# Chunk 0 prepared ahead of the last one-hot groups, and sorted rows turned by products with the identity

## What is computed

```python
xn = layernorm(x)
# branch 1: tokens sorted by nearest of 8 means, then a selective scan over the sorted order
buckets = argmax(l2norm(xn) @ l2norm(means).T);  sort_idx = argsort(buckets, stable=True)
u = xn[sort_idx].T
x_dbl = x_proj_weight @ u                       # 32 rows dts, 16 rows B, 16 rows C
C = x_dbl[48:] + (means @ prompt_weight.T)[sorted bucket].T
delta = softplus(dt_projs_weight @ dts + dt_projs_bias)
h = exp(delta * A) * h + (delta * u) * B;  y = sum_n(h * C) + D * u     # 16 states a channel
# branch 2: top-2 of 8 experts, each silu(xn @ w1) * (xn @ w3) @ w2
out = x + unsort(y) + experts(xn)
```

## Time and profile before

| | before |
|---|---|
| three runs, median (lowest to highest) | 813.2 us (810.62 to 814.56) |
| the profiled execution | 809.9 us, span 808.1 us |
| VectorE busy | 681.9 us, 84% of the span |
| TensorE busy | 656.6 us, 81% |
| GpSimd busy | 595.9 us, 74% |
| ScalarE busy | 420.7 us, 52% |
| granted TensorE clock, mean of the span | 0.914 of full speed |
| moved by DMA | 116.97 MB, mean 145 GB/s |

### The profile page before, as it was taken

The page is one execution under the profiler, slowest core; times in us unless marked ns, Lnnn a source line. Parts: engine busy times, 40 slices in busy tenths (PEclk is TensorE's granted clock), DMA queues, the critical chain, the costliest instruction groups (busy, mean ns, idle before and its releaser), DMA issues.

```text
span 808.1 us, 13714 instructions
## 1 busy us (share of the span) xinstructions
PE 656.6 (81%) x4538; PEld 422.3 (52%) x4538; DVE 681.9 (84%) x883; ACT 420.7 (52%) x910; POOL 595.9 (74%) x371
## 2 busy tenths in 40 slices
PE   2733879558988799987989898899879888989991
PEld 1423734225655465555656555565546555655661
DVE  5868767679999999999999999999989999997120
ACT  1323666546655565565555665566546555652320
POOL 3727810055698899898989998898989899898442
PEclk9955965588999999999999999999999999999996
DMA  7982568999835744674475456556536754433231
GB/s 205 370 285 91 167 215 276 294 304 258 187 87 114 172 108 92 145 167 92 107 155 118 107 131 144 118 118 144 128 78 147 158 106 100 89 61 45 47 40 20
DMA packets 66275, 116.97 MB, mean 145 GB/s; under 512 B 12104, under 2 KB 46496, under 8 KB 64160
## 3 DMA queue, kind: packets, MB, share of 16 engines
q1 hardware_dynamic: 44048, 88.78, 39.0%
q0 software_dynamic: 19824, 27.16, 19.6%
q10 hardware_dynamic: 2336, 0.15, 0.2%
HBM read 80.78 MB, written 35.27 MB: 144 GB/s over the span
## 4 chain that ended last, share of the span: by engine, by line
DVE 52%; POOL 13%; PE 11%; issue 11%; DMA 9%; ACT 2%; SPq 1%; another core or an unknown queue 0%; DVEq 0%; POOLq 0%; ACTq 0%
DVE ring L957 29%; DVE pb L948 14%; POOL ring L462 5%; DMA out_dram<-pool,tab 4%; DVE pool L986 4%; POOL out_dram L456 3%; PE fa L1097 2%; PE fb L1113 2%; POOL out_dram L449 2%; DMA ring<-in_L_attn_x_dram 2%; POOL w2x L425 1%; PE py L1204 1%; POOL pool L442 1%; DMA late<-dd_d 1%; DMA dd_d<-ring 1%
## 5 line engine op out<-in xcount | busy, mean ns | idle before, releaser
L462 POOL TENSOR_TENSOR ring<-ring,bc 128x1024 f32<-128x1024 f32 (+1 forms) x127 | 305.9, 2428 | 25.0 <-DVE state L964 22.5
L957 DVE TENSOR_TENSOR_SCAN ring<-ring,state,pb 128x512 f32<-128x512 f32 x256 | 313.8, 1267 | 5.8 <-ACT ring L606 1.3
L606 ACT ACTIVATE ring<-late,aneg 128x512 f32<-128x512 f32 x256 | 164.6, 728 | 13.1 <-DMA late<-dd_d 10.8
L948 DVE TENSOR_TENSOR pb<-fb,bc 128x1024 f32<-128x1024 f32 x128 | 157.3, 1229 | 5.1 <-ACT fb L617 2.9
L449 POOL DMA_INDIRECT out_dram<-pool,tab x71 | 113.5, 1599 | 42.5 <-DMA out_dram<-pool,tab 19.5
L1193 PE MATMUL fa<-w,pool 128*128 x284 | 135.1, 598 | 10.6 <-ACT pool L664 10.6
L1204 PE MATMUL py<-w2x,pool 128*128 x568 | 141.2, 394 | 0.0
L1193 PE MATMUL fb<-w,pool 128*128 x284 | 133.5, 592 | 0.0
L442 POOL DMA_INDIRECT pool<-xn_d,tab x71 | 71.3, 1005 | 78.6 <-DVE ids L914 34.3
L1204 PEld LDWEIGHTS py<-w2x,pool 128*128 128x128 f32 x568 | 108.0, 201 | 13.0
L1126 PE MATMUL py<-ring,fold 128*32 128x128 f32 x2048 | 69.4, 276 | 24.8 <-POOL ring L462 24.8
(11 more groups left out here) (211 smaller groups left out, 750.3 us busy)
## 6 DMA issues: line engine op xcount, KB each, us to landing
late<-dd_d SPq DMA_DIRECT2D x256, 128.0 KB
bc<-bc_d SPq DMA_DIRECT2D x64, 256.0 KB
w<-in_L_ffn_w_dram SPq DMA_DIRECT2D x16, 512.0 KB, 8.1
ring<-in_L_attn_x_dram SPq DMA_DIRECT2D x8, 512.0 KB, 4.5
out_dram<-ring SPq DMA_DIRECT2D x8, 512.0 KB, 6.9
xn_d<-w2x SPq DMA_DIRECT2D x8, 512.0 KB, 8.1
dd_d<-pool SPq DMA_DIRECT2D x8, 512.0 KB, 3.3
dd_d<-ring SPq DMA_DIRECT2D x8, 512.0 KB, 4.7
```

Of the source, the lines that this page charges most:

```text
L462: return po.tensor_tensor(r, r, bc[:, u // G % 2, 1, states, :].rearrange("p n c -> p (n c)"), ALU.mult)
L606: ins = ac.activation(ring[:, u % RING, n, :], dd[:, u % 2, 0, :], ACT.Exp, scale=aneg[:, NH * g + n:NH * g + n + 1])
L948: ve.tensor_tensor(pb[:, :].rearrange("p (n c) -> p n c", n=2), pd[:, :].rearrange("p (o c) -> p o c", o=1).to_broadcast([P, 2, CH]), bc[: ...
L957: ve.tensor_tensor_scan(r, r, pb[:, CH * m:CH * m + CH], state[:, NH * g + n:NH * g + n + 1], ALU.mult, ALU.add).then_inc(S["scan_done"], 1)
```

## The change

The order of TensorE's list changes: chunk 0 is turned ahead of invert(5), invert(6) and invert(7) go behind project_delta(0) and project_delta(1). ScalarE's and VectorE's lists follow it: weigh(7) stands behind the logarithms of chunk 0, the table of experts inside chunk 0's prepare, slot_table behind chunk 1. turn_rows issues ordinary products with the identity instead of transposes. Two of the three places of ut are exchanged, so that the last chunk's lies behind ring's first slot, and exps(0) waits for less. SyncE loads the first two experts' weights at c = 2 and 3, units 0 and 1 at c = 4, the other weights from unit 2 on behind that unit's rows, and its wait for all stores moves to unit 3.

```diff
-        ut = [v.rearrange("p (k c) -> p k c", k=KC) for v in (pool[:, 1032:2056], flat[:, 1032:2056], flat[:, 6144:7168])]
+        ut = [v.rearrange("p (k c) -> p k c", k=KC) for v in (pool[:, 1032:2056], flat[:, 6144:7168], flat[:, 1032:2056])]
...
                 store_dd(c)
-                if c == NCH // 2 - 1:
+                if c == 2:
+                    sp.wait_ge(S["bc_put0"], 32)
                     sp.wait_ge(S["tab_ready"], 1)
...
-                if NCH // 2 <= c < NCH // 2 + EARLY:
-                    load_up(c - NCH // 2, w3, w3_in)
-                    load_down(c - NCH // 2)
-                if c == 2:
-                    sp.wait_ge(S["bc_put0"], 32)
-                if 2 <= c < 2 + P // DG:
-                    load_bc(0, c - 2)
-                if c == 5:
+                if 2 <= c < 2 + EARLY:
+                    load_up(c - 2, w3, w3_in)
+                    load_down(c - 2)
+                if c == 4:
                     for h in range(KC):
                         sp.wait_ge(S[f"dd_put0{h}"], 16)
                     load_dd(0)
                     load_dd(1)
-
-            for n in range(KC * 2):
-                sp.wait_ge(S[f"dd_put{n // 2}{n % 2}"], 16 * NCH // 2)
-            for n in range(2):
-                sp.wait_ge(S[f"bc_put{n}"], 32 * NCH // 2)
+                if 2 <= c < 2 + P // DG:
+                    load_bc(0, c - 2)
...
                 if u >= 2:
                     load_dd(u)
-                if c == 0 and g + EARLY < E:
-                    load_up(g + EARLY, w3, w3_in)
-                    load_down(g + EARLY)
+                if c == 0 and EARLY <= g:
+                    load_up(g, w3, w3_in)
+                    load_down(g)
+                if u == 3:
+                    for n in range(KC * 2):
+                        sp.wait_ge(S[f"dd_put{n // 2}{n % 2}"], 16 * NCH // 2)
+                    for n in range(2):
+                        sp.wait_ge(S[f"bc_put{n}"], 32 * NCH // 2)
...
                 if u == 0:
+                    ac.wait_ge(S["pr_tr"], NCH)
+                    ac.wait_ge(S["pr_ids"], NCH)
+                    ac.wait_ge(S["pr_du"], KC * (NCH - 2))
+                elif u == 1:
                     ac.wait_ge(S["pr_du"], KC * NCH)
-                elif u == 1:
...
-            for g in range(NGRP - 1):
+            for g in range(NGRP - 2):
                 weigh(g)
             take_u(0)
-            weigh(NGRP - 1)
+            weigh(NGRP - 2)
             take_x(0)
...
                 softplus_ln(c)
+                if c == 0:
+                    weigh(NGRP - 1)
...
+            evac_xt(0)
             put_du(0)
             exps(0)
-            evac_xt(0)
+            tanh(0)
             exps(1)
             for u in range(1, FT + 1):
                 j = u - 1
-                tanh(j)
+                if j:
+                    tanh(j)
...
+                if c == 0:
+                    expert_table()
                 if c + 2 < NCH:
                     cluster_rows(c + 2)
...
                 if g in (4, 6):
                     cluster_rows(g // 2 - 2)
...
-            take_ids(0)
+                if g == NGRP - 2:
+                    take_ids(0)
             for c in range(NCH):
                 prepare(c)
-                if c == 0:
+                if c == 1:
                     slot_table()
...
-                        ins = pe.transpose(rows_ps[c % 2][k][:, P * t:P * t + P], prep[c % 2]["xsr"][:, t, P * k:P * k + P],
-                                           ident[:, :])
+                        ins = pe.matmul(rows_ps[c % 2][k][:, P * t:P * t + P], prep[c % 2]["xsr"][:, t, P * k:P * k + P],
+                                        ident[:, :], start=True, stop=True)
...
-            for g in range(NGRP - 2):
+            for g in range(NGRP - 3):
                 invert(g)
             turn_rows(0)
-            invert(NGRP - 2)
+            invert(NGRP - 3)
             for c in range(NCH):
                 project(c)
-                if c == 0:
-                    invert(NGRP - 1)
                 if c < NCH - 1:
                     turn_rows(c + 1)
                 project_delta(c)
+                if c < 2:
+                    invert(NGRP - 2 + c)
```

More of the change, by code:

```diff
@@ L964, in keep_states, with expert_table @@
                 ve.tensor_reduce(state[:, NH * g:NH * g + NH], ring[:, u % RING, :, CH - 1:CH], AX, ALU.max).then_inc(S["h_ready"], 1)
+            def expert_table():
+                last = NB - 1
+                link(ve.tensor_tensor(ge[:, :, 0:last], jt.rearrange("p (j o) -> p j o", o=1).to_broadcast([1, FTP, last]),
+                                      ct[0:1, 0:last].rearrange("p (o k) -> p o k", o=1).to_broadcast([1, FTP, last]), ALU.is_ge))
+                link(ve.tensor_reduce(etf, ge[:, :, 0:last], AX, ALU.add))
+                link(ve.tensor_copy(etab[:, :], etf))
             for g in range(NGRP):
@@ L969, in _ @@
                     cluster_rows(g // 2 - 2)
-            last = NB - 1
-            link(ve.tensor_tensor(ge[:, :, 0:last], jt.rearrange("p (j o) -> p j o", o=1).to_broadcast([1, FTP, last]),
-                                  ct[0:1, 0:last].rearrange("p (o k) -> p o k", o=1).to_broadcast([1, FTP, last]), ALU.is_ge))
-            link(ve.tensor_reduce(etf, ge[:, :, 0:last], AX, ALU.add))
-            link(ve.tensor_copy(etab[:, :], etf))
-            take_ids(0)
+                if g == NGRP - 2:
+                    take_ids(0)
             for c in range(NCH):
                 prepare(c)
-                if c == 0:
+                if c == 1:
                     slot_table()
```

## The result

The changed kernel takes 806.3 us (median of 13 runs, 803.7 to 810.3), the kernel before 811.7 us (13 runs beside it, 807.7 to 816.4). The ratio is 0.9937, 95% interval 0.9917 to 0.9956: 5.1 us saved by the ratio (the medians lie 5.4 apart), where 14.2 were predicted. Its profiled execution took 807.84 us, with a span of 806.1 us; that is only 2.1 us under the profiled execution of the kernel before, as single executions of one kernel lie up to 6.6 us apart here.

What follows compares the result with a forecast made beforehand. TensorE at half clock bounded the preparation, DMA second, VectorE the long scan stage; 9.3 us from unit 0's start plus 4.9 from closed gaps made 14.2, so 795.7 us profiled, 799.0 median, range 794 to 810.

Steps and rivals of the forecast that it cites:

- rival one: Preparation: the 4.3 us stall recurs or the beat stays near 7.3 us; gain only 7 to 11 us; chance 0.17.
- rival three: Preparation: half clock, the stall, and TensorE waiting about 3 us for rows queued behind weights; slower, 817 us; chance 0.06.
- The gaps behind unit 0: Between units 0 and 2: reordered waits and loads bring unit 2's rows early and close gaps, 4.9 us.
- The start of unit 0: End of preparation: DMA sets unit 0's start, at about 151.6 instead of 160.88, 9.3 us gained.
- from about 114.5 us on the queue is full: Preparation: with weights moved to chunks 2 and 3, DMA transfers are counted on from 114.5 us at 310 GB/s.
- Order of groups: Early preparation: moved one-hot groups start project(2) at about 105.4 instead of 109.87; 4.4 us without the stall, nearly nothing with it.
- Price of the products: TensorE's turning by products: 1.74 us a chunk at full clock, 3.5 at half, against 0.87 and 1.90 by transposes.
- The clock: Preparation: longer turnings by products bring full clock back within a chunk or two where it falls, and mostly keep it.
- The beat: Preparation: at full clock TensorE needs 4.5 us a chunk instead of 7.31, and the bound passes to VectorE at 5.28.
- What the clock is worth: Preparation: products lose 0.9 or 1.6 us a chunk at equal clock and pay only by the clock; DMA is the next limit.
- Rows behind weights: Preparation: rows of chunks 6 and 7 queue behind 2.6 MB of weights and stores; TensorE waits about 3 us.
- What a start of unit 2 is worth: Scan stage: every microsecond by which unit 2 starts earlier should be one off the end; 14.2 us counted.

Runs made afterwards that it cites:

- b_tail: The kernel before with only the part behind the preparation (ut places, exps waits, tanh(0), SyncE's store wait, later weights): 808.2 us, ratio 0.9949.
- b_product: The kernel before with products with the identity instead of transposes in turn_rows, nothing else changed: 811.5 us, ratio 1.0014.
- a_early4: The changed kernel with four experts' weights instead of two loaded ahead of the units, at chunks 2 to 5: 806.4 us, ratio 1.0039 to the kernel before.
- a_late: The changed kernel with the first two experts' weights behind the stores of chunks 6 and 7: 802.97 us, ratio 1.0002 to the kernel before.
- a_transpose: The changed kernel with transposes again in turn_rows, all else as changed: 806.9 us, ratio 0.9936 to the kernel before.
- a_early1: The changed kernel with one expert's weights instead of two ahead of the units, at chunk 4: 807.2 us, ratio 0.993 to the kernel before.
- a_late_transpose: a_late with transposes instead of products in turn_rows: 801.6 us, ratio 0.9978 to the kernel before.
- a_weights45: The changed kernel with the first two experts' weights at chunks 4 and 5, as before the change: 807.0 us, ratio 0.9951 to the kernel before.
- a_early1_transpose: a_early1 with transposes instead of products in turn_rows: 804.3 us, ratio 0.9895 to the kernel before.
- after_again: The changed kernel, unchanged, repeated on another chip beside the kernel before: 807.0 us, ratio 0.9937.
- b_hold_scatter: The kernel before with GpSimd's last six scatters held until ScalarE has copied chunk 1: 811.3 us in one run.

## Why the prediction was right or wrong

The sign was right and the time inside the range, but the gain was 5.1 us where 14.2 were forecast. It is less than rival one's 7 to 11 us: that rival's stall came, and rival three's waits for rows with it. Step by step:

*The gaps behind unit 0, 4.9 us: right.* From unit 0 to unit 2 it takes 5.4 us less, unit 0 itself came 0.3 us later, and there is no idle ahead of unit 2. b_tail, which holds this part alone, has a ratio of 0.9949 against 0.9937. (The forecast's units add up to 168.6 for unit 2, not 168.9; that is 0.3 us.)

*The start of unit 0, 9.3 us: wrong, it gave nothing.* That the transfers set this point was right: 4.2 MB moved it by 14.3 us, and b_product made TensorE 6.3 us earlier and gained no time. The rate of 310 GB/s was right too (311 measured). The step that failed is "from about 114.5 us on the queue is full". The first weights were issued at 123.64, 9.1 us later, and the share was 0.13 at 114 to 116. Counted on from there, 151.6 + 9.1 = 160.7, and unit 0 started at 161.22. Each mark of the count came late by about as much: the rows of chunk 6 at 134.4 (counted: 124.7), those of chunk 7 at 144.5 (135), VectorE's chunk 7 at 156.60 (147.3). This chunk also waited for the second half of the store, which adds 0.55 us:

```profile
157.90 0.75 DVE L931 TENSOR_SCALAR ring<-pt,dtb 128x512 f32<-128x512 f32 x1 [0.55 <-DMA dd_d<-ring]
```

In bytes: from 114.5 to unit 0 the queue moved 13.9 MB (46.7 us at 298 GB/s), where the count has 11.5 (7.7 us more at 310 GB/s), and up to 123.64 it moved them at 237 GB/s, a share of 0.69 (2.2 us). So work that the count had behind it at 114.5 was still to come.

The 9.1 us have two parts, parted by a_early4, which has the same issues up to there but no stall: it issued its first weights at 117.56. So some 3.1 us are the count's own, which came too early even where project(2) came as walked, and some 6.1 us are the stall and what followed it. This parting compares two chips and is rough: the midpoint of unit 0 in a_late and a_early4, 156.4, would make it 4.8 and 4.8. The changed kernel itself did not run on B.

*Order of groups, 4.4 us if the stall goes, nothing if it stays: right as a condition, wrong as a choice.* project(0) at 90.64 (walked: 91.1), project_delta(0) at 94.22 (94.5), and on chip B project(2) at 105.63 (105.4). With the stall of 4.57 us project(2) came at 111.71, 1.8 us later than before, since invert(7) now stands right behind the stall and took 3.96 us at half clock instead of 1.96. The sum took the stall as gone, although nothing in the change removes it; rival one said so, with 0.17. That is the second fault: what was unexplained should have been kept in the sum.

*Price of the products: close.* Predicted 1.74 us a chunk at full clock and 3.5 at half, measured 1.98 to 2.05 and 3.78. Both are nearer to the uncut group (1.96 and 3.9), which stood as the upper bound. project_delta, taken as 1.2, was 1.42.

*The clock: right in what it did, in part by luck.* It was full from 111.4 to 131.9 and came back behind each turning at half clock, at 138.7 and 149.0. But the rise at 111.4 came at the end of invert(7), 3.96 us of products that the stall had left at half clock, and a_transpose has it too; the forecast expected rises from the turnings. The later rises are theirs, as in b_product, and so is that it stayed: in the changed kernel it fell only where TensorE stood waiting, with transposes also while TensorE was at work (a_transpose, near 125), and there it did not come back before 166. "Each rise in this trace" was read too narrowly: the prediction's own next paragraph has a rise at 43 us behind transposes.

*The beat: right.* VectorE's was 5.20 us without idle, against 5.28 predicted, and the chain runs over VectorE from 114.4 to 128.3. TensorE started a chunk every 4.99 us, where 4.5 was predicted: 1.60 us of project, 1.98 of turning, 1.42 of delta.

*What the clock is worth: overrated in the sum, though the text knew the next limit.* Products and transposes differ by nothing that can be told in three pairs (b_product and the kernel before, a_transpose and the changed kernel by their ratios, the a_late pair on B), and in the fourth, a_early1 on C, the transposes lead by 2.9 us with overlapping intervals. The rule on transposes in the Trainium skill (Perfetto Trace Analysis, Transposes) loses nothing here: at full clock a turning takes 1.98 us by products and 1.02 by transposes, from its start to that of the next piece (a_late_transpose, 92.56 to 93.58). The other rule of the Trainium skill, that transposes do not count as busy for the clock (TensorE: Matmul & The Clock Gate, Part 4), fits a_late and a_late_transpose better than the prediction granted. But the turning by transposes is also the shorter piece of work (1.90 against 3.78 us at half clock), and these runs don't part the two readings. A full clock lasted 13 us with turnings by transposes (a_transpose, 112 to 125), but it then fell with no wait above 0.57 us before it, which speaks for the page too.

*Rows behind weights: rival three's mechanism came true, its price did not.* TensorE waited 6.08 and 3.02 us for the rows of chunks 6 and 7, three times what I gave it. It cost next to nothing, as a_weights45 shows: without most of that wait unit 0 started 0.9 us earlier, as the next transfers stood right behind, and the time was the same.

*What a start of unit 2 is worth.* I carried it to the end one to one. That is right on the average: from unit 2's first scan to the end of the span the four profiles with the earliest unit 2 have 625.2 us and the four with the latest 625.0, so the scan stage gives nothing back. But a single profile lies anywhere from 622 to 628, and the place of unit 2 scatters too. a_early1_transpose's unit 2 is 6.9 us ahead of after_again's, and their profiled executions are 7.0 us apart; the medians are only 2.8 apart, as the one profiled was 2.5 us faster than its kernel's median and the other 1.8 us slower.

## What to carry to other kernels

Where a stage ends with a full DMA queue, count the bytes that lie ahead of the first transfer the next stage needs, and from when the queue is really full. Speeding up the engines ahead of it here mostly lengthened their waits; bytes taken out or put behind moved it (and helped where they weren't needed at once). An unexplained stall that a change does not touch belongs in the sum, with what stands right behind it priced at the clock the stall leaves. Undo each part of a change by itself: here a wait moved and a few loads reordered held all of the gain that can be told, and a 32% shorter beat of TensorE none. And a position read from one profile isn't a median.

## What was unexpected in the hardware

On chips A, C and D, and in both first profiles, each kernel has a stall of 1.6 to 4.9 us at 100 to 107 us, in which TensorE or ScalarE waits for a releaser that the profile can't name ("remote"), or for nothing that it shows. The four kernels profiled on chip B had none. The place and the size don't follow the order of groups or the kind of turning; the cause is open.

The same kernel took 803.0 us on chip B and 811.9 to 813.6 on the others, 1.1 to 1.3%, twice what the change is worth. On B the stall is missing. Whether that is all of the difference was not measured, but it may be: b_hold_scatter, whose TensorE lost its clock in a wait there, took 811.3. The best changed variant on B reached 0.9978, with unit 2 at 178.31, about where the estimate above puts the kernel before. So the gain of 5 us may hold only on chips with the stall; the changed kernel did not run on B.

TensorE 13.89 of 14 us busy with transposes, project and products over few rows kept half clock for as long as it lasted (a_late_transpose). In the eight profiles with products, each turning of eight blocks that ran at half clock, 3.6 to 3.8 us, was followed by full clock, but for one: in a_weights45 it took a second turning, as the prediction's "within a chunk or two" allows.
